# Masked attention, first stage: the high part of the keys cast by ScalarE, the subtraction a slot later, and key stores ahead of key loads

## Chip, cores and metric

One core of a Trainium2 chip (trn2) runs the whole program in one launch. The metric is the device time of one execution in microseconds (us), as the median of several runs.

## The reference, cut to what matters

Eight stages follow each other, each adding to x (32 sequences of 56 rows, width 128). The first one is a cross-attention over 1500 keys a sequence, with 16 heads of width 8, a bias and a mask:

```python
x = x + tanh(g_xattn[0]) * L0_xattn_ref(layernorm(x), ctx, ctx, mask, bias, W_q, b_q, W_k, b_k, W_v, b_v, W_o, b_o)
# in it, for every head: NaN and infinities of q, k, v and the bias are replaced by 0, 10000 and -10000,
# scores = q @ k.T / sqrt(8) + bias, masked keys get -10000, softmax over the keys, times v, times W_o
```

The kernel multiplies q and k to float32's accuracy with bfloat16 operands: q and k are each split into three bfloat16 parts (high, middle, low), and six products of parts are packed into one matmul of 96 rows (`K_PART`, `Q_PART`).

## The kernel before, in words

The change lies in `masked_attention`, the first stage. Its five engines each run a list written out by hand; semaphores order them against each other. The work goes in slots: slot p of sequence n, with p from 0 to 7, treats a pair of heads. In this text "score 4.1" is the scores of slot 4, second half of the keys; "shift 4.1" is VectorE's pass over them; and so on.

What a slot does:
- TensorE: score p.0 (L1017, L1019), transposes of the probabilities' arguments of slot p - 2 (`turn`, L1029), score p.1, more transposes, then one piece of other work: the key projections of sequence n + 2 in slots 0 to 2 (`keys`, L973), the value projections in slots 3 to 5 (`values`, L979), weighted sums (L1042, L1055) in most slots. Score p.h waits for shift (p - 1).h, since the PSUM tile of each half is used again.
- VectorE: shift p.0 (L1310: bias added and the row maximum taken), work on the keys and values of sequence n + 2, shift p.1, more such work, and the negated maximum (L1318).
- ScalarE: three exponentials of slot p - 2 (`exp`, L1141), two subtractions of the maximum (`lower`, L1130), and in slots 0 to 2 the copy of a third of the keys out of PSUM (`keep`, L1124).
- GpSimd: a list with no slots of its own (L945 to L958): guard 0, guard 1, split 0, guard 2, split 1, guard 3, split 2, blocks, guard 4, guard 5. A guard clamps a third of the keys (0 to 2) or of the values (3 to 5) in three operations, L916, L917, L919. A split makes the middle and low part of a third of the keys (L926, L928). `blocks` (L894) lays out the queries.
- SyncE: it issues all DMAs from one queue, in the order of L851 to L872; a wait in it holds all that stands behind.

How a third i of the keys of sequence n + 2 goes on its way, before the change: `keys` (slot i) on TensorE, `keep` on ScalarE, guard i on GpSimd and beside it the finite test `finite` on VectorE (L1257), then `take_keys` in slot i + 2 on VectorE, in one piece: copy i (L1263, the copy under the finite mask), the cast to the high part (L1268), and the subtraction of it, "rest i" (L1270). Before the cast it waits for `k_stored`, since `k_parts` has two buffers for the three thirds: the buffer of third 2 is that of third 0, which must have been stored. Then comes split i, which waits for rest i, then store i (L814), then the loads that pack the keys for the scores (L825), two packed rows at a time, each paced by a count of scores. The packed keys of a half are first read one sequence later.

In slots 2 to 7 VectorE also takes over the values (L1257, L1278, L1285; "copy 3" to "copy 5" below are the values' copies of L1285 in slots 5 to 7, and "copy 4" is that of slot 6, behind guard 4), compares the mask (L1240, slots 0, 2 and 4) and normalises sequence n - 1 (L1338 to L1344, slot 6).

Of the kernel before, what the change touches and what calls it, by code (L numbers as in the profile page):

```python
# [20 lines left out]
ACT = mybir.ActivationFunctionType  # L21
# [673 lines left out]
def masked_attention(nc, g, name, a, w):  # L695
# [4 lines left out]
    with r.ctx:  # L700
# [84 lines left out]
        with nc.Block() as block:  # L785
            @block.sync
            def _(sp):
# [23 lines left out]
                def store_keys(n, i):  # L811
                    at = 3 * n + i
                    sp.wait_ge(low_ready, at + 1)
                    sp.dma_start(a["k_scratch"][n % 2].rearrange("a f k -> f a k")[:, :, third(i)],  # L814
                                 k_parts[:, at % 2, :, :]).then_inc(k_stored[at % 2], 16)
# [35 lines left out]
                for n in range(B):  # L851
                    if n + 1 < B:
                        load_keys(n + 1, 0, (0, 1))
                        load_mask(n + 1, 1)
                        load_keys(n + 1, 0, (2, 3))
                    load_mask_t(n)
                    if n + 1 < B:
                        load_mask(n + 1, 2)
                        load_keys(n + 1, 0, (4, 5))
                    if n > 1:  # L860
                        sp.wait_ge(y_copied, n - 1)
                        sp.dma_start(a["y_scratch"][:, (n - 2) * S:(n - 1) * S], y_now).then_inc(y_stored, 16)
                    for i in range(3):
                        if n + 1 < B:
                            load_keys(n + 1, 1, (2 * i, 2 * i + 1))
                        if n + 2 < B:
                            store_keys(n + 2, i)
                        if n + 3 < B:
                            load_ctx(n + 3, i)
                    if n + 2 < B:  # L870
                        load_mask(n + 2, 0)
                        load_queries(n + 2)  # L872
# [238 lines left out]
            def _(act):  # L1111
# [6 lines left out]
                def keep(n, i):  # L1118
                    at = 3 * n + i
                    act.wait_ge(k_turned, at + 1)  # L1120
                    if at == 0:
                        act.wait_ge(q_ready, NQ)
                    wait(act, k_ready, at - 1)
                    act.activation(raw_k[:, at % 2, :], side[:, 0:THIRD], ACT.Identity, bias=bk[:]).then_inc(raw_k_ready, 1)  # L1124

                def lower(n, p, h):
                    at = n * HP + p
                    act.wait_ge(neg_ready, at + 1)
                    some = logits[at % 3][:, h * HALF:(h + 1) * HALF]
                    act.activation(some, some, ACT.Identity, bias=neg_top[:, n % 2, p:p + 1]).then_inc(lowered, 1)  # L1130
# [32 lines left out]
                    wait(act, y_stored, 16 * n)  # L1163
                    act.activation(y_now, side[:, 0:S], ACT.Identity, bias=bo[:]).then_inc(y_copied, 1)

                for i in range(3):
                    keep(0, i)
                count(0)
                for i in range(3):
                    keep(1, i)  # L1170
                for n in range(B):
                    for p in range(HP):
                        prior = (n, p - 2) if p > 1 else (n - 1, p + HP - 2)
                        last = (n, p - 1) if p > 0 else (n - 1, HP - 1)
                        if p == 0 and n > 1:
                            finish(n - 2)
                        for t in range(3):
                            if prior[0] >= 0:
                                exp(*prior, t)
                            if t < 2 and last[0] >= 0:  # L1180
                                lower(*last, t)
                            if t == 1 and p < 3 and n + 2 < B:
                                keep(n + 2, p)
                        if p == 1 and n > 0:
                            weigh_share(n - 1)
                        if p == 4 and n > 0:
                            mix(n - 1)
                        if p == 5 and n + 1 < B:
                            count(n + 1)
# [11 lines left out]
            def _(dve):  # L1201
# [57 lines left out]
                def take_keys(n, i):  # L1259
                    at = 3 * n + i  # L1260
                    dve.wait_ge(rough_ready, 6 * n + i + 1)
                    dve.wait_ge(good_ready, 6 * n + i + 1)
                    dve.copy_predicated(clean_k[at % 2], good[:, (6 * n + i) % 2, 0:THIRD],  # L1263
                                        raw_k[:, at % 2, :]).then_inc(k_ready, 1)
                    dve.wait_ge(k_ready, at + 1)
                    if at > 1:
                        dve.wait_ge(k_stored[at % 2], 16 * (at // 2))
                    dve.tensor_copy(k_parts[:, at % 2, 0, :], clean_k[at % 2]).then_inc(high_ready, 1)  # L1268
                    dve.wait_ge(high_ready, at + 1)
                    dve.tensor_tensor(clean_k[at % 2], clean_k[at % 2], k_parts[:, at % 2, 0, :],  # L1270
                                      ALU.subtract).then_inc(rest_ready, 1)
# [77 lines left out]
                for n in (0, 1):  # L1349
                    for i in range(3):  # L1350
                        finite(n, i)
                        take(n, i)
                    for b in range(3):
                        keep_values(n, b)
                        finite(n, b + 3)
                        take(n, b + 3)
                    if n == 0:
                        for i in range(3):
                            mark(0, i)
                        clean_bias()  # L1360
                        floors(0)
                for n in range(B):
                    for p in range(HP):
                        shifted(n, p, 0)
                        if p > 1 and n + 2 < B:
                            take(n + 2, p - 2)
                        if 0 < p < 7 and n + 2 < B:
                            finite(n + 2, p - 1)
                        if p in (0, 2, 4) and n + 1 < B:
                            mark(n + 1, p // 2)  # L1370
                        if p == 5:
                            mark_t(n)
                        shifted(n, p, 1)
                        if 3 <= p < 6 and n + 2 < B:
                            keep_values(n + 2, p - 3)
                        if p == 0 and n > 0:
                            share_of(n - 1)
                        if p == 5 and n > 0:
                            add_masked(n - 1)
                        if p == 6 and n > 0:  # L1380
                            normalise(n - 1)
                        if p == 7 and n + 1 < B:
                            floors(n + 1)
                        negate(n, p)
# [1239 lines left out]
```

## Time and profile before

| what | value |
|---|---|
| median of 3 runs | 6507.41 us (6505.57 to 6512.12) |
| time of the profiled execution | 6505.09 us |
| its span | 6503.3 us |
| mean granted TensorE clock | 0.915 |
| busy: TensorE, VectorE, ScalarE, GpSimd | 5399.5, 4556.5, 3155.4, 1967.3 us |
| the loop of the changed stage, first to last shift | 161.7 to 1550.1 us |

The profile is that of one execution. Busy times are sums over all eight stages; the loop of the stage that the change touches is a fifth of the span. In the timelines below a row has the start in us from the beginning of the span, the duration in us, the engine, the line, the operation, what it writes and reads, and, in brackets, how long the engine stood idle just before it and who ended that.

### The profile page before, as it was taken

The page shows a single profiled execution, that of the slowest core. Times are in us where ns is not written, and L with a number is a line of the kernel's source. Part 1 is how long each engine was busy: PE and PEld are TensorE (multiplying, and loading weights), DVE is VectorE, ACT ScalarE, POOL GpSimd, SP SyncE. Part 2 cuts the span into 40 slices and gives each one's busy share as a digit, 9 for nine tenths or more (in the row PEclk, how much of TensorE's full clock was granted, in tenths as well). Part 3 has the DMA queues.
Part 4 walks back from the last instruction along what each step waited for, and adds up shares of the span by engine and source line. Part 5 has one row for each costly group of instructions (what it writes and reads, how often), then busy time and mean ns, then how long its engine had stood idle before and what let it go on. Part 6 is the DMA issues. An engine that isn't in the chain of part 4 may idle for free. (4 is left out here: it accounts for less than half of the span.)

```text
span 6503.3 us, 132525 instructions
## 1 busy us (share of the span) xinstructions
PE 5399.5 (83%) x51199; PEld 3938.7 (61%) x51199; DVE 4556.5 (70%) x9168; ACT 3155.4 (49%) x5932; POOL 1967.3 (30%) x1458
## 2 busy tenths in 40 slices
PE   2898898896599999955947999999999658888887
PEld 1777777775277777745933444444444437777775
DVE  6888888885177777751446777777777448778774
ACT  0666666664165555531224444444444225555552
POOL 4766766761122222201011111111110023333330
PEclk6999999998699999977978999999999769999998
DMA  4555555552366666631010000000000068888870
GB/s 109 124 121 125 122 121 125 122 120 54 75 120 131 133 129 126 132 87 50 23 27 25 15 19 14 14 19 14 14 19 4 5 128 148 143 150 150 146 138 10
DMA packets 368260, 544.58 MB, mean 84 GB/s; under 512 B 115654, under 2 KB 247880, under 8 KB 367390
## 3 DMA queue, kind: packets, MB, share of 16 engines
q1 hardware_dynamic: 365678, 533.44, 39.8%
q8 instruction: 378, 6.19, 0.5%
q0 software_dynamic: 2048, 3.67, 0.2%
q14 instruction: 156, 1.28, 0.1%
HBM read 413.08 MB, written 123.90 MB: 83 GB/s over the span
## 5 line engine op out<-in xcount | busy, mean ns | idle before, releaser
L635 DVE CUSTOM_DVE_ANT_0 attn_logits<-attn_scores,attn_shift 112x750 f32<-112x750 f32 x1024 | 943.5, 931 | 468.4 <-PE attn_scores L452 467.7
L555 ACT ACTIVATE attn_probs_t<-attn_pt 125x448 f32<-125x448 f32 x1536 | 831.2, 542 | 780.4 <-PE attn_pt L467 760.3
L467 PEld LDWEIGHTS attn_pt<-ident,attn_logits 112*125 112x125 f32 x6144 | 867.0, 191 | 222.3 <-issue 80.7
L467 PE MATMUL attn_pt<-ident,attn_logits 112*125 112x112 f32 x6144 | 926.2, 274 | 67.8 <-DVE attn_logits L649 42.1
L2241 PE MATMUL attn2k_pk<-attn_wk,attn2k_cn_t 128*125 128x512 f32 x1536 | 737.9, 602 | 39.5 <-ACT attn2k_cn_t L2312 36.7
L2252 PE MATMUL attn2k_pg<-attn2k_kn,attn2k_cn 125*128 125x512 f32 x1536 | 725.0, 594 | 4.5 <-ACT attn2k_gram L2320 2.3
L2407 DVE TENSOR_REDUCE attn2k_ss<-attn2k_sq 125x16 f32<-125x1024 f32 x384 | 467.0, 1216 | 255.4 <-ACT attn2k_sq L2349 255.3
L389 POOL CAST attn_k_parts<-xn_t 128x500 bf16<-128x500 f32 x192 | 199.4, 1039 | 1407.4 <-DVE xn_t L605 1407.3
L1141 ACT ACTIVATE attn_probs_t<-attn_pt 125x448 f32<-125x448 f32 x768 | 414.8, 540 | 308.5 <-PE attn_pt L1029 305.9
L2349 ACT ACTIVATE attn2k_sq<-attn2k_pk 125x1024 f32<-125x1024 f32 x384 | 391.9, 1021 | 326.3 <-PE attn2k_pk L2241 326.2
L452 PE MATMUL attn_scores<-attn_k_packed,attn_q_blocks 96*112 96x375 bf16 x2048 | 523.3, 338 | 24.6 <-POOL attn_q_blocks L379 17.9
L2241 PEld LDWEIGHTS attn2k_pk<-attn_wk,attn2k_cn_t 128*125 128x125 f32 x1536 | 274.1, 187 | 399.3 <-issue 296.9
L1017 PE MATMUL attn_scores<-attn_k_packed,attn_q_blocks 96*112 96x375 bf16 x1024 | 357.2, 349 | 149.3 <-DVE attn_tops L1310 149.3
L2419 DVE TENSOR_TENSOR attn2k_kn<-attn2k_pk,attn2k_rn 125x1024 f32<-125x1024 f32 x384 | 470.1, 1224 | 13.3
L2252 PEld LDWEIGHTS attn2k_pg<-attn2k_kn,attn2k_cn 125*128 125x128 f32 x1536 | 264.1, 192 | 298.2 <-issue 286.3
L1310 DVE CUSTOM_DVE_ANT_0 attn_logits<-attn_scores,attn_bias,attn_floor 112x750 f32<-112x750 f32 x342 | 337.9, 988 | 101.8 <-PE attn_scores L1019 100.2
L649 DVE TENSOR_SCALAR attn_logits<-attn_logits,attn_neg_top 112x1500 f32<-112x1500 f32 x320 | 375.5, 1173 | 0.1
L480 PE MATMUL attn_po<-attn_probs_t,attn_v 125*32 125x112 f32 x12288 | 371.7, 272 | 1.3 <-ACT attn_probs_t L555 1.3
L1130 ACT ACTIVATE attn_logits<-attn_logits,attn_neg_top 112x750 f32<-112x750 f32 x342 | 312.9, 916 | 113.7 <-DVE attn_neg_top L1318 111.6
L2223 POOL COPY attn2k_q_now<-attn_q_t 128x448 f32 (+1 forms) x32 | 17.8, 558 | 1135.4 <-PE attn2k_pz L2273 1135.4
L546 ACT ACTIVATE attn_logits<-attn_logits,attn_neg_top 112x750 f32<-112x750 f32 x384 | 351.2, 915 | 10.5 <-DVE attn_neg_top L643 8.8
L421 PE MATMUL attn_side<-attn_ctx_t,attn_wk 128*128 128x500 f32 x384 | 219.7, 655 | 152.8 <-DVE xn_t L605 86.1
(360 smaller groups left out, 10814.0 us busy)
## 6 DMA issues: line engine op xcount, KB each, us to landing
attn_k_packed<-k_scratch SPq DMA_DIRECT2D x384, 375.0 KB, 5.9
attn_k_packed<-k_scratch SPq DMA_DIRECT2D x384, 187.5 KB, 3.9
k_scratch<-attn_k_parts SPq DMA_DIRECT2D x64, 1125.0 KB, 7.4
attn_ctx_t<-in_ctx_t SPq DMA_DIRECT2D x64, 750.0 KB, 7.3
k_scratch<-attn_k_parts SPq DMA_DIRECT2D x96, 375.0 KB, 4.5
attn_ctx_t<-in_ctx_t SPq DMA_DIRECT2D x96, 250.0 KB, 4.6
attn2k_ctx<-in_ctx SPq DMA_DIRECT2D x32, 750.0 KB
attn_mask_in<-in_mask SPq DMA_DIRECT2D x192, 109.4 KB
```

What stands on the lines that cost most here:

```text
L452: last = pe.matmul(scores[h][0:PAIR, b, 0:QTR], q_blocks[:, n % 2, p, :, :].rearrange("p a s -> p (a s)"), k_packed[:, n % 2, p, h * HALF ...
L467: last = pe.transpose(pt[(3 * at + t) % 2][0:KC, (c % 4) * PAIR:(c % 4 + 1) * PAIR], logits[:, at % 3, c * KC:(c + 1) * KC], g.ident[0:PAI ...
L480: last = pe.matmul(po[32 * j:32 * j + 32, grp * PAIR:(grp + 1) * PAIR], v[:, n % 3, c, V1 * p:V1 * p + 32], probs_t[0:KC, grp, c, j * PAIR ...
L555: act.activation(probs_t[0:KC, p // 4, 4 * t:4 * t + 4, (p % 4) * PAIR:(p % 4 + 1) * PAIR], pt[(3 * at + t) % 2][0:KC, 0:QUAD].rearrange(" ...
L635: dve.tensor_tensor_reduce(out=logits[:, at % 3, cols].rearrange("p (b k) -> p b k", b=2), in0=scores[h][0:PAIR, :, 0:QTR], in1=shift[:, n ...
L649: dve.tensor_scalar(at, at, neg_top[:, n % 2, p:p + 1], None, ALU.add).then_inc(dve_lowered, 1)
L1141: act.activation(probs_t[0:KC, at % PV_RING, 4 * t:4 * t + 4, :], pt[(3 * at + t) % 2][0:KC, 0:QUAD].rearrange("p (c q) -> p c q", c=4), A ...
L2241: last = pe.matmul(pk[c % 2][0:KC, b, :], cn_t[:, c % 2, :], wk[:, b * HW:(b + 1) * HW], start=True, stop=True)
L2252: last = pe.matmul(pg[:, b, :], cn[:, j, c, :], kn[:, c % 2, b * HW:(b + 1) * HW], start=(c == 0), stop=(c == CH - 1))
L2349: act.activation(sq[:, c % 2, :].rearrange("p (a b) -> p a b", a=2), pk[c % 2][0:KC, :, :], ACT.Square).then_inc(sq_ready, 1)
L2407: dve.tensor_reduce(ss[:, c % 2, :], sq[:, c % 2, :].rearrange("p (h d) -> p h d", h=H2), AX.X, ALU.add).then_inc(ss_ready, 1)
L2419: dve.tensor_tensor(kn[:, c % 2, :].rearrange("p (h d) -> p h d", h=H2), pk[c % 2][0:KC, :, :].rearrange("p a (h d) -> p (a h) d", h=8), r ...
```

## The change

In `take_keys`, VectorE's cast and the wait for `k_stored` ahead of it go away. A new function `high` does both on ScalarE, with an activation of type Copy; in the loop it stands at the end of slots 2, 3 and 4, after the third exponential. VectorE's subtraction becomes a function of its own, `rest`, and stands behind shift p.0 in slots 3, 4 and 5, ahead of the copy of that slot: one slot later than before. In the prologue ScalarE's list is laid out anew, with the same idea. On SyncE, store i of sequence n + 2 goes ahead of the two key loads of sequence n + 1 with which it shares a step of the loop.

```diff
@@ sync
                     for i in range(3):
+                        if n + 2 < B:
+                            store_keys(n + 2, i)
                         if n + 1 < B:
                             load_keys(n + 1, 1, (2 * i, 2 * i + 1))
-                        if n + 2 < B:
-                            store_keys(n + 2, i)
                         if n + 3 < B:
                             load_ctx(n + 3, i)
@@ scalar
+                def high(n, i):
+                    at = 3 * n + i
+                    act.wait_ge(k_ready, at + 1)
+                    if at > 1:
+                        act.wait_ge(k_stored[at % 2], 16 * (at // 2))
+                    act.activation(k_parts[:, at % 2, 0, :], clean_k[at % 2], ACT.Copy).then_inc(high_ready, 1)
...
-                for i in range(3):
-                    keep(0, i)
-                count(0)
-                for i in range(3):
-                    keep(1, i)
+                for n in (0, 1):
+                    keep(n, 0)
+                    keep(n, 1)
+                    high(n, 0)
+                    keep(n, 2)
+                    high(n, 1)
+                    high(n, 2)
+                    if n == 0:
+                        count(0)
...
+                        if 2 <= p < 5 and n + 2 < B:
+                            high(n + 2, p - 2)
@@ vector
-                    dve.wait_ge(k_ready, at + 1)
-                    if at > 1:
-                        dve.wait_ge(k_stored[at % 2], 16 * (at // 2))
-                    dve.tensor_copy(k_parts[:, at % 2, 0, :], clean_k[at % 2]).then_inc(high_ready, 1)
+
+                def rest(n, i):
+                    at = 3 * n + i
                     dve.wait_ge(high_ready, at + 1)
                     dve.tensor_tensor(clean_k[at % 2], clean_k[at % 2], k_parts[:, at % 2, 0, :],
                                       ALU.subtract).then_inc(rest_ready, 1)
...
                         take(n, i)
+                        rest(n, i)
...
                         shifted(n, p, 0)
+                        if 3 <= p < 6 and n + 2 < B:
+                            rest(n + 2, p - 3)
                         if p > 1 and n + 2 < B:
                             take(n + 2, p - 2)
```

## Rows read from the trace of the kernel before

**Rows 1.** The page, part 1: busy time, share of the span, instructions.
```profile
PE 5399.5 (83%) x51199; PEld 3938.7 (61%) x51199; DVE 4556.5 (70%) x9168; ACT 3155.4 (49%) x5932; POOL 1967.3 (30%) x1458
```

**Rows 2.** Windows: length, busy of PE, PEld, DVE, ACT, POOL, granted clock; one sequence.
```profile
850.70:856.40 5.70, 5.64 (x36) 4.88 (x36) 5.57 (x11) 3.02 (x5) 5.62 (x5) 0.50 0.32 95
...
sum 44.30, PE 39.55 PEld 33.95 DVE 37.52 ACT 28.96 POOL 30.32; mean PE 7.91 PEld 6.79 DVE 7.50 ACT 5.79 POOL 6.07
```

**Rows 3.** Waits, 400 to 1400 us: us in total, times, longest.
```profile
PE attn_scores L1017 <- DVE attn_tops L1310: 110.5, 67, 4.4
...
DVE attn_k_parts L1268 <- DMA k_scratch<-attn_k_parts: 40.2, 23, 2.4
```

**Rows 4.** Timeline of TensorE: scores 2.0, 3.0, 5.1, then 0.1, 3.0 of the next.
```profile
831.16 0.37 PE L1017 MATMUL attn_scores<-attn_k_packed,attn_q_blocks 96*112 96x375 bf16 x1
...
836.00 0.37 PE L1017 MATMUL attn_scores<-attn_k_packed,attn_q_blocks 96*112 96x375 bf16 x1
...
850.76 0.56 PE L1017 MATMUL attn_scores<-attn_k_packed,attn_q_blocks 96*112 96x375 bf16 x1 [3.84 <-DVE attn_tops L1310]
...
866.83 0.32 PE L1017 MATMUL attn_scores<-attn_k_packed,attn_q_blocks 96*112 96x375 bf16 x1
...
880.31 0.37 PE L1017 MATMUL attn_scores<-attn_k_packed,attn_q_blocks 96*112 96x375 bf16 x1
```

**Rows 5.** Timeline of VectorE, slots 2 to 7 of the same sequence.
```profile
832.05 1.00 DVE L1310 CUSTOM_DVE_ANT_0 x_sb<-attn_scores,attn_bias,attn_floor 112x750 f32<-112x750 f32 x1 [2.14 <-PE attn_scores L1019]
...
833.75 1.31 DVE L1268 CAST attn_k_parts<-attn_clean_late 128x500 bf16<-128x500 f32 x1
...
840.82 1.47 DVE L1257 TENSOR_SCALAR attn_good<-xn_t 128x500 int32<-128x500 f32 x1
...
844.77 0.97 DVE L1263 COPY_PREDICATED attn_clean_late<-attn_good,xn_t 128x500 f32<-128x500 int32 x1
847.26 0.75 DVE L1268 CAST attn_k_parts<-attn_clean_late 128x500 bf16<-128x500 f32 x1 [1.51 <-DMA k_scratch<-attn_k_parts]
...
849.71 0.98 DVE L1310 CUSTOM_DVE_ANT_0 attn_logits<-attn_scores,attn_bias,attn_floor 112x750 f32<-112x750 f32 x1
...
851.35 0.98 DVE L1310 CUSTOM_DVE_ANT_0 x_sb<-attn_scores,attn_bias,attn_floor 112x750 f32<-112x750 f32 x1
...
858.73 0.77 DVE L1285 COPY_PREDICATED attn_v<-attn_good,y_t 125x512 f32<-125x512 int32 x1
...
865.16 0.98 DVE L1310 CUSTOM_DVE_ANT_0 attn_logits<-attn_scores,attn_bias,attn_floor 112x750 f32<-112x750 f32 x1
```

**Rows 6.** Line L1268, whole stage: durations in ns, min/median/max, first and last start.
```profile
L1268 DVE CAST attn_k_parts<-xn_t x48: 420/472/1321, 49.6 to 1461.0; 128x500 bf16<-128x500 f32 x48
```

**Rows 7.** Timeline of ScalarE: key copy and last exponentials of slots 2 and 4.
```profile
835.02 0.68 ACT L1124 ACTIVATE xn_t<-attn_side,attn_bk 128x500 f32<-128x500 f32 x1
835.58 0.55 ACT L1141 ACTIVATE attn_probs_t<-attn_pt 125x448 f32<-125x448 f32 x1
...
846.03 0.53 ACT L1141 ACTIVATE attn_probs_t<-attn_pt 125x448 f32<-125x448 f32 x1
```

**Rows 8.** Timeline of SyncE's queue: store 0.
```profile
842.85 0.42 SPq L814 DMA_DIRECT2D k_scratch<-attn_k_parts  x1
```

**Rows 9.** Timeline of GpSimd: split 0, ends of guards 2 and 3, split 2, end of guard 4.
```profile
835.84 0.72 POOL L926 CAST attn_k_parts<-attn_clean_late 128x500 bf16<-128x500 f32 x1 [1.06 <-DVE attn_clean_late L1270]
...
840.73 1.29 POOL L919 TENSOR_TENSOR attn_clean_late<-attn_clean_late,y_t 128x500 f32<-128x500 f32 x1
...
846.55 1.18 POOL L919 TENSOR_TENSOR attn_v<-attn_v,y_t 125x512 f32<-125x512 f32 x1
...
848.79 0.73 POOL L926 CAST attn_k_parts<-attn_clean_late 128x500 bf16<-128x500 f32 x1 [1.06 <-DVE attn_clean_late L1270]
...
855.45 1.19 POOL L919 TENSOR_TENSOR attn_v<-attn_v,y_t 125x512 f32<-125x512 f32 x1
```

**Rows 10.** Line L1270, whole stage: durations in ns, min/median/max, first and last start.
```profile
L1270 DVE TENSOR_TENSOR xn_t<-xn_t,attn_k_parts x48: 678/680/1489, 50.3 to 1461.5; 128x500 f32<-128x500 f32 x48
```

## The prediction

> **What bounds the kernel now.** The page comes first. TensorE is busy 83% of the span, VectorE 70% [rows 1]; that average mixes eight stages, and the change touches one, the first attention with its 32 sequences. So the page can't price it. The windows over one of its sequences can: 44.30 us, in which TensorE is busy 39.55, VectorE 37.52, GpSimd 30.32 and ScalarE 28.96 [rows 2]. No engine is full, so a chain through several of them sets the period. The waits say where it breaks: score matmuls (L1017) waited 110.5 us in 1000 us for VectorE's shift pass, and VectorE's cast waited 40.2 us, 23 times, for the key store to land [rows 3].
>
> The timelines of one sequence give the chain. Score 3.0 (slot 3, first half) starts at 836.00 and again at 880.31, a period of 44.31. From 821.4 to slot 5 TensorE runs almost through; then it stands 3.84 us until score 5.1 at 850.76 [rows 4], and the granted clock is at its lower level, 0.50 (1.2 of 2.4 GHz), for the next 5.7 us [rows 2]. It stood for shift 4.1, which VectorE began at 849.71 only, because it had waited 1.51 us for the store, then cast for 0.75 and subtracted for 0.68 [rows 5]. After score 5.1 TensorE runs without a gap to score 3.0 of the next sequence, the last 13.48 us of it from score 0.1 at 866.83. Shift 7.1, which score 0.1 needs, ended at 866.14 [rows 4, 5]: VectorE's second chain has only 0.69 us to spare. That slack matters below.
>
> **The change, part by part.** Only the 30 sequences that prepare keys for n + 2 change.
>
> *Cast off VectorE.* Three casts a sequence, 0.42 us at the least and 1.32 at the most, median 0.47 [rows 6], and the store's wait of 1.51. In slot 4 it is 1.51 + 0.75 = 2.26 us ahead of shift 4.1, and the subtraction beside it moves in front of the copy. In slot 2 the gain is smaller than it looks: the cast lasted 1.31 instead of 0.42 because it started under a GpSimd operation [rows 5], and the finite test that now takes its place would start under the same one and end at the same 835.06. The mask compare then takes 0.4, and shift 2.1 starts at 835.4 instead of 836.76, so score 3.1 waits no longer.
>
> *Cast on ScalarE.* No row has it. The nearest is the key copy L1124, also 128x500, at 0.68 us [rows 7]; below, VectorE's own 0.42 [rows 6]; I take 0.65. Three are 1.95 us on an engine that is idle 15 us of 44.30. Each stands behind the last exponential of its slot: high 0 comes when that ends at 836.13, and high 2, whose exponential ends at 846.56 [rows 7] (about 845.2 after the change, since slot 4 begins earlier), when copy 2 is done at 845.7. Each is done well before its subtraction in the next slot; what queues behind high 2 is the mix and exp 3.0, at most 0.65 us later, while TensorE stands waiting for shift 4.1. Cost zero. Without that cover it would be at most 0.65 a sequence.
> The Trainium skill (ScalarE: Activation LUTs, What ACT_TABLE_LOAD costs) gives an ACTIVATE with immediate scale and bias 186 ns plus 0.833 ns an element, an estimate of 0.60 us here, which would change nothing in the sum.
>
> *Stores ahead of loads.* SyncE issued store 0 at 842.85, behind two key loads that are paced by the scores; the cast could go on at 847.26, 4.41 later [rows 8, 5]. Now it goes when the low part is ready, at about 840.6 by the next step, and lands at 845.0, before high 2 at 845.7 wants its buffer. Loads 4 and 5 may wait up to 1 us longer behind store 2, but slot 4 of the next sequence is some 40 us away. Cost zero, gain already counted.
>
> *The subtraction a slot later.* This is what costs. Shift 3.0 starts 0.89 after score 3.0, as shift 2.0 did (831.16 to 832.05 [rows 4, 5]): 836.89. Rest 0 ends 0.91 + 0.68 later, at 838.48, and GpSimd can begin split 0 at 838.54 instead of 835.84 [rows 9]: 2.70 late. GpSimd's order is fixed: split 0, guard 2, split 1, guard 3, split 2, blocks, guard 4. That took 835.84 to 856.64, less an idle of 1.06: 19.74 us of work [rows 9]. Before, the guards had room; now they follow on each other:
> - guard 2 ends at 842.02 + 2.70 = 844.72, so copy 2 in slot 4 starts at 844.8, where it stood before (844.77). It ends at 845.7; finite test and mask compare then cost 0.42 each alone and up to 1.47 beside GpSimd [rows 5]. Between 846.8 and 848.2 for shift 4.1, I take 847.9: 1.8 us gained.
> - Shift 5.0 follows 1.64 later (849.71 to 851.35 [rows 5]), 849.5; rest 2 could start at 850.4, just when guard 3 makes its last, two-input operation (846.55 to 847.73 before [rows 9], now about 849.4 to 850.6). A subtraction took 1.49 at the most, against a median of 0.68 [rows 10], and the long ones are those of the prologue that met such an operation. So rest 2 ends between 851.1 and 851.9, and GpSimd, free at 850.5, waits 0 (if shift 4.1 comes early) to 1.4 us; I take 0.9.
> - guard 4 ends at 838.54 + 19.74 + 0.9 = 859.2, and copy 4 starts at 859.3. It started at 858.73 [rows 5]: 0.57 late. VectorE had gained 1.8 and loses all of it at this point.
> - Copy 4 to the end of shift 7.1 took 7.41 [rows 5]. Guard 5 now runs beside the normalisation: 0 to 0.5 more, I take 0.2. Shift 7.1 ends at 866.91, score 0.1 starts at 866.98, score 3.0 another 13.48 later, at 880.46.
>
> **Sum.** 880.46 - 836.00 = 44.46 against 44.31: +0.15 us, times 30 is +4.5 us. The profiled execution took 6505.1 us, so 6509.6 for one like it; the median of the three runs lies 2.3 above it: 6512. All that the edits save goes into the 0.69 us of slack and into GpSimd's later start.
> Bounds: without any collision and wait, copy 4 is at 858.35, the period 43.3, that is -1.0 x 30 = -30 us: 6477. With GpSimd waiting 1.4, 0.5 more inside its operations and 0.5 in the normalisation, the period is 45.7, +1.4 x 30 = +42: 6549.
>
> The row on the subtraction is mixed: 1.49 at the most, yet 0.68 in the median [rows 10]; but then most ran while GpSimd waited for them, so it says little of a GpSimd that is always busy. The Trainium skill (SBUF — State Buffer, Who interferes with whom) has VectorE and GpSimd share one port pair as an exclusive lock, a two-input VectorE operation meeting any GpSimd operation that reads. By that rule rest 1 and rest 2 are both held, and the time is that of the slower case below; the longest subtraction speaks for it, the median neither way.
>
> **The rivals.**
> - *Faster, chance 0.25.* VectorE's two-input and fast operations fall between GpSimd's, shift 4.1 comes at 846.8 and rest 2 is done before GpSimd asks. Then the period is 43.3 to 43.8. For it: 40.2 us of waits and all the casts are truly gone. Against: GpSimd is busy without a gap for 20 us, so collisions are hard to miss. About 43.6, -0.7 x 30: 6486.
> - *GpSimd does not bind at all, 0.05.* Then shift 4.1's full 2.26 comes through, -68 us: 6440. Against it is the fixed order.
> - *Slower, 0.30: GpSimd's chain in slot 6.* Place: copy 4 waits for guard 4. Price: every us that rest 0 or rest 2 comes late, times 30. It decides once copy 4 starts after 859.2, since 0.69 less the 0.2 for normalisation is used up at that time. With a period of 45.1, +0.8 x 30: 6531.
> - *A second low clock, 0.04.* TensorE could reach score 7.1 at 860.1 and waits for shift 6.1 until 861.3; if that idle brings the lower level again where TensorE sets the end, it costs as in [rows 2] half of 5.7 us, 86 us in all: 6598. Idles of 0.5 did not do it, 3.84 did.
> - *The wait only moves*: if store 0 landed after 845.7, ScalarE would wait instead. Rest 2 has 4 us of room for it, so it is worth nothing and is part of the forecast.
>
> **How the numbers follow.** About 0.2% (13 us) can be told from no change, that is 0.43 us a sequence. My forecast, a period within that of 44.31, has 0.36 and gives 6512 (its own range 6495 to 6520). The two faster cases make 0.30, the two slower 0.34. The range 6477 to 6549 leaves out the non-binding case, the second clock fall and the tails, under 0.2 together.
>
> **What would show it.** In the changed profile: no wait of VectorE on the store; casts of 0.6 to 0.68 on ScalarE; shift 4.1 1 to 3 us earlier against score 3.0; GpSimd without idle from split 0 to guard 4, and split 0 about 2.5 us later; a new wait of VectorE in slot 6 before copy 4, on GpSimd; TensorE's wait before score 5.1 down to some 3 us, and a new one before score 7.1 or 0.1. I am wrong if copy 4 does not wait (then faster), if score 0.1 waits over 0.6 us (then slower), or if the low clock stretch goes or doubles.

## The result, and the profile after

The changed kernel took **6583.69 us** (median of 4 runs, 6577.45 to 6589.56), against 6509.76 for the kernel before beside it: a ratio of **1.0111**, 95% interval 1.0097 to 1.0125. That is 1.1% slower and above the range of the prediction (6477 to 6549). The profiled execution took 6577.45 us, its span is 6575.6.

The 72.3 us by which the span grew (6575.6 less 6503.3) lie in the changed stage. VectorE's smallest mask operation (L1245 before, L1258 after) runs once a sequence, in slot 5. From its first to its last run it was 1349.6 us before and is 1423.3 now, 73.7 more. Before, 29 sequences took 44.31 us each on average. Now the shortest take 46.0, and 9 take 46.4. Another 7 take 47.9, the first 46.7, and the step after these 29 takes 39.3 instead of 31.9. So 49 us come from the sequences' shortest period (29 x 1.69), 17.4 from the longer ones, 7.3 from the last step.

The busy times hardly changed (compare [rows 1]). Page, part 1, after:

```profile
PE 5430.0 (83%) x51199; PEld 3956.7 (60%) x51199; DVE 4553.7 (69%) x9072; ACT 3195.5 (49%) x6028; POOL 2006.0 (31%) x1458
```

For VectorE that evenness hides something. Windows from the first to the last shift, before and after (columns as in [rows 2]):

```profile
161.70:1550.10 1388.40, 1239.33 (x18758) 1063.99 (x18762) 1158.75 (x2313) 913.01 (x1546) 912.57 (x751) 0.92 0.53 119
162.30:1623.00 1460.70, 1267.95 (x18764) 1080.26 (x18768) 1159.82 (x2224) 947.13 (x1636) 950.79 (x751) 0.93 0.55 113
```

Before, 68.9 of VectorE's 1158.8 us were its 90 casts. They are gone, and it is still busy 1159.8 us: its other operations became about 70 us longer in all. GpSimd, with the same operations, is busy 38 us longer. So the change added more than idle time: operations of both engines grew.

Windows over one sequence of 46.0 us, from score 3.0 to the next one (the columns are those of [rows 2]):

```profile
840.30:847.10 6.80, 6.72 (x40) 5.68 (x41) 6.80 (x11) 4.10 (x6) 6.03 (x5) 0.52 0.80 152
847.10:854.20 7.10, 5.18 (x76) 4.42 (x74) 4.97 (x13) 3.84 (x8) 6.74 (x6) 1.00 0.94 180
...
sum 46.00, PE 40.44 PEld 34.22 DVE 37.33 ACT 30.17 POOL 31.64; mean PE 6.74 PEld 5.70 DVE 6.22 ACT 5.03 POOL 5.27
```

The lower clock (0.52) is still there in slot 5. In this sequence it lasts 6.8 us, as it did before in every one (now it is 3.4 in most of the others, there or in slot 6), and VectorE is busy through all of it. In the 7.1 us behind it, slot 6, VectorE works for only 4.97 and TensorE for 5.18, while GpSimd works for 6.74. One of the sequences of 47.9 us has the lower clock (0.56 on average) in another place too, from about where its score 7.1 starts (430.47), after a wait of 1.96 us:

```profile
429.60:436.40 6.80, 5.93 (x62) 5.11 (x63) 6.66 (x13) 2.56 (x4) 2.85 (x2) 0.56 0.14 33
```

The waits from 400 to 1400 us say who is waited for (us in total, times, longest):

```profile
PE attn_scores L1017 <- DVE attn_tops L1322: 123.9, 60, 2.9
POOL attn_k_parts L926 <- DVE xn_t L1282: 48.3, 22, 3.8
POOL attn_k_parts L926 <- DVE attn_clean_late L1282: 47.8, 22, 3.8
DVE attn_v L1297 <- POOLq L921: 44.0, 21, 2.1
DVE xn_t L1276 <- POOLq L921: 16.4, 11, 1.5
```

VectorE's wait for the key store, 40.2 us in [rows 3], is gone. In its place VectorE waits for GpSimd: 2.1 us ahead of every copy 4 (L1297) and 1.5 us ahead of every copy 2 (L1276). TensorE's wait for the shift grew from 110.5 to 123.9.

The same sequence in the timelines. TensorE, scores 3.0, 5.1, 7.1, 0.1 and the next 3.0:

```profile
827.86 0.37 PE L1017 MATMUL attn_scores<-attn_k_packed,attn_q_blocks 96*112 96x375 bf16 x1
...
840.38 0.56 PE L1017 MATMUL attn_scores<-attn_k_packed,attn_q_blocks 96*112 96x375 bf16 x1 [2.92 <-DVE attn_tops L1322]
...
854.25 0.37 PE L1017 MATMUL attn_scores<-attn_k_packed,attn_q_blocks 96*112 96x375 bf16 x1 [1.96 <-DVE attn_tops L1322]
...
860.37 0.32 PE L1017 MATMUL attn_scores<-attn_k_packed,attn_q_blocks 96*112 96x375 bf16 x1
...
873.84 0.37 PE L1017 MATMUL attn_scores<-attn_k_packed,attn_q_blocks 96*112 96x375 bf16 x1
```

VectorE: shift 3.0, rests 0 and 1, copy 2, shift 4.1, rest 2, a mask operation, copy 4, one step of the normalisation, shift 7.1:

```profile
828.75 1.00 DVE L1322 CUSTOM_DVE_ANT_0 attn_logits<-attn_scores,attn_bias,attn_floor 112x750 f32<-112x750 f32 x1 [0.35 <-PE attn_scores L1019]
829.67 0.68 DVE L1282 TENSOR_TENSOR xn_t<-xn_t,attn_k_parts 128x500 f32<-128x500 f32 x1
...
834.55 0.68 DVE L1282 TENSOR_TENSOR attn_clean_late<-attn_clean_late,attn_k_parts 128x500 f32<-128x500 f32 x1
836.72 0.72 DVE L1276 COPY_PREDICATED xn_t<-attn_good,xn_t 128x500 f32<-128x500 int32 x1 [1.50 <-POOLq L921]
...
839.33 0.99 DVE L1322 CUSTOM_DVE_ANT_0 x_sb<-attn_scores,attn_bias,attn_floor 112x750 f32<-112x750 f32 x1
...
841.89 1.68 DVE L1282 TENSOR_TENSOR xn_t<-xn_t,attn_k_parts 128x500 f32<-128x500 f32 x1
...
844.87 1.44 DVE L1258 TENSOR_SCALAR attn_out_t<-attn_out_t 125x672 f32<-125x672 int32 x1
...
851.80 0.77 DVE L1297 COPY_PREDICATED attn_v<-attn_good,y_t 125x512 f32<-125x512 int32 x1 [2.10 <-POOLq L921]
...
855.69 0.87 DVE L1352 TENSOR_TENSOR xn_t<-attn_mixed,xn_t 128x224 f32<-128x224 f32 x1
...
859.09 0.97 DVE L1322 CUSTOM_DVE_ANT_0 x_sb<-attn_scores,attn_bias,attn_floor 112x750 f32<-112x750 f32 x1
```

GpSimd: split 0, the long step of guard 2, split 1, the end of guard 3, split 2, the end of guard 4:

```profile
830.41 1.00 POOL L926 CAST attn_k_parts<-xn_t 128x500 bf16<-128x500 f32 x1 [3.80 <-DVE xn_t L1282]
...
833.42 1.88 POOL L917 TENSOR_SCALAR xn_t<-xn_t 128x500 f32<-128x500 f32 x1
...
836.80 1.06 POOL L926 CAST attn_k_parts<-attn_clean_late 128x500 bf16<-128x500 f32 x1 [0.17 <-POOL xn_t L919]
...
841.85 1.18 POOL L919 TENSOR_TENSOR attn_v<-attn_v,y_t 125x512 f32<-125x512 f32 x1
843.63 1.04 POOL L926 CAST attn_k_parts<-xn_t 128x500 bf16<-128x500 f32 x1 [0.60 <-DVE xn_t L1282]
844.75 1.19 POOL L928 TENSOR_TENSOR attn_k_parts<-xn_t,attn_k_parts 128x500 bf16<-128x500 f32 x1
...
850.53 1.19 POOL L919 TENSOR_TENSOR attn_v<-attn_v,y_t 125x512 f32<-125x512 f32 x1
```

GpSimd stands still for 3.80 us until rest 0 is done, then works to the end of guard 4 at 851.72, with one wait on VectorE, 0.60 us for rest 2. Copy 4 starts 0.08 us after that end.

The two moved pieces did what they were meant to. The cast on ScalarE, whole stage (ns, min/median/max), and store 0 on SyncE's queue:

```profile
L1131 ACT ACTIVATE attn_k_parts<-xn_t x48: 621/626/635, 50.2 to 1528.2; 128x500 bf16<-128x500 f32 x48
```

```profile
832.72 0.38 SPq L814 DMA_DIRECT2D k_scratch<-attn_k_parts  x1
```

### The profile page after: what moved, and what is told of

Same layout as the page of the kernel before. It is cut to its first block and busy times, and to the rows that moved or that the text cites. A ratio compares the mean times of both kernels' runs of the same rounds, so it can differ in the third digit from the quotient of the medians.

```text
span 6575.6 us, 132525 instructions
## 1 busy us (share of the span) xinstructions
PE 5430.0 (83%) x51199; PEld 3956.7 (60%) x51199; DVE 4553.7 (69%) x9072; ACT 3195.5 (49%) x6028; POOL 2006.0 (31%) x1458
```

## The experiments

The theories, as the expectations name them. **A**: GpSimd's fixed list starts a slot later, because the subtraction does, and comes out too late at copy 4. **B**: the stores' new place on SyncE's queue costs (SyncE waits for the low part with loads behind it). **C**: ScalarE's cast holds up the exponentials. **D**: the cost lies in the collisions of VectorE and GpSimd, each lengthening the other's operations, and not in the date at which GpSimd starts.

"VectorE's cast" below is the cast of the kernel before, "late" is the subtraction one slot later. Ratios are against runs of the kernel before on the same chip (medians 6510.65 to 6512.86).

**One part alone: the store order.** The kernel before with each store ahead of the two key loads. Since the subtraction stays early, store 0 now could overwrite packed keys that are still being read, so SyncE also waits for that read ahead of store 0.

```diff
                     for i in range(3):
+                        if n + 2 < B:
+                            if i == 0:
+                                sp.wait_ge(k_in[(2 * n + 1) % 3], ((2 * n + 1) // 3 + 1) * NPART * 16)
+                            store_keys(n + 2, i)
                         if n + 1 < B:
                             load_keys(n + 1, 1, (2 * i, 2 * i + 1))
-                        if n + 2 < B:
-                            store_keys(n + 2, i)
```

> The kernel before with SyncE's order alone changed (store i ahead of its two key loads; one wait for key loads that were done some 30 us earlier is added ahead of store 0). Theory A, GpSimd's list begins a slot later because of the late subtraction: this part is innocent; VectorE's wait of 1.5 us before the cast of slot 4 goes, shift 4.1 comes up to 1.5 us earlier, GpSimd's list is not later, so the time is between no change and -45 us (1.5 x 30): about 6490. Theory B, the stores' waits hold SyncE's queue and the key loads come late: slower than before, up to the full +73 us, with waits of score matmuls on key loads in the trace. Theory C, ScalarE's cast holds the exponentials: no part of it is here, so as theory A.

Measured: 6464.93 us, ratio 0.9927 (0.9908 to 0.9946). It is **faster than both kernels**, and theory B falls. The wait for the store is gone and GpSimd's list still starts early. Waits, 400 to 1400 us:

```profile
PE attn_scores L1019 <- DVE attn_tops L1312: 94.7, 75, 3.0
...
POOL attn_k_parts L928 <- DVE xn_t L1272: 12.7, 12, 1.1
```

TensorE waits 94.7 us where it was 110.5 [rows 3], and no wait of VectorE for GpSimd appears.

**The other part alone: the subtraction a slot later.** The kernel before, stores in their old place, cast on VectorE.

```diff
+                def rest(n, i):
+                    at = 3 * n + i
                     dve.wait_ge(high_ready, at + 1)
...
                         shifted(n, p, 0)
+                        if 3 <= p < 6 and n + 2 < B:
+                            rest(n + 2, p - 3)
```

> The kernel before with the subtraction alone moved a slot later; the cast stays on VectorE in the slot of the copy, the stores stay behind the loads. Theory A: slower than before, by at least as much as the changed kernel, since VectorE keeps its casts and its waits: +60 to +120 us, 6570 to 6630, with VectorE waiting for GpSimd before copy 2 (slot 4) and copy 4 (slot 6). Theory B and theory C: within 0.3% of before, since neither ScalarE nor SyncE's order is touched; a store's wait may even be shorter.

Measured: 6591.91 us, ratio 1.0131 (1.0106 to 1.0155). This one edit costs as much as the whole change. The same waits stand there as after the change: VectorE's for GpSimd ahead of copy 4 in the same amount (44.0 us), GpSimd's for the rests somewhat longer (112.5 us against 96.1):

```profile
POOL attn_k_parts L926 <- DVE attn_clean_late L1273: 56.9, 33, 3.8
POOL attn_k_parts L926 <- DVE xn_t L1273: 55.6, 32, 3.8
DVE attn_v L1288 <- POOLq L921: 44.0, 21, 2.1
```

**The change with the subtraction back in its slot.** Cast on ScalarE behind the second `lower` of the slot, rest i in slot i + 2 behind the finite test and the mask, ahead of shift p.1; the same wait ahead of store 0.

```diff
-                        if 3 <= p < 6 and n + 2 < B:
-                            rest(n + 2, p - 3)
...
+                        if 2 <= p < 5 and n + 2 < B:
+                            rest(n + 2, p - 2)
```

> The changed kernel with the subtraction back in the slot of its copy, behind the finite test and the mask compare and ahead of the second shift; ScalarE casts one step earlier in its slot, after the second lowering (and the one extra wait for key loads as in the store order alone). Theory A: GpSimd starts split 0 within about 1 us of the kernel before, copies 2 and 4 wait no longer, and VectorE is rid of cast and store wait: faster than before by 0.5 to 2 us a sequence, 6450 to 6495. Theory B and theory C: cast on ScalarE and store order are both in it, so it stays as slow as the changed kernel, about 6580.

Measured: 6519.88 us, ratio 1.0018 (1.0007 to 1.0029). A miss for A as it was put: the change's loss is gone, the gain of the store order isn't there. ScalarE's way round is longer than VectorE's own cast, so split 0 is still 1.1 us later than before against shift 3.0 (table below). VectorE waits for GpSimd again:

```profile
DVE attn_v L1299 <- POOLq L923: 61.4, 46, 2.1
```

**The layout of the queries behind the guards.** The changed kernel, with GpSimd's `blocks` after guards 4 and 5, so that guard 4 is free to end earlier.

```diff
-                    if n + 1 < B:
-                        blocks(n + 1)
                     if n + 2 < B:
                         guard(n + 2, 4)
                         guard(n + 2, 5)
+                    if n + 1 < B:
+                        blocks(n + 1)
```

> The changed kernel with GpSimd's blocks operation (1.7 to 1.9 us, needed only by the next sequence) moved behind guards 4 and 5. Theory A: guard 4 ends some 1.9 us earlier, VectorE's wait of 2.1 us before copy 4 goes to about 0.2, and the period falls by 1.0 to 1.9 us: 30 to 57 us off the changed kernel, 6525 to 6555. Theory B and theory C: GpSimd is not the bound, the time stays at about 6582 within 0.2%.

Measured: 6604.3 us, ratio 1.0130 (1.0107 to 1.0154). A miss, and not for want of the first effect: copy 4's wait fell from 2.10 to 0.44. But the layout now meets the normalisation, whose second two-input step (L1354, 0.39 us after the change) waits it out. Timeline of VectorE, then of GpSimd, then of TensorE:

```profile
855.37 0.81 DVE L1297 COPY_PREDICATED attn_v<-attn_good,y_t 125x512 f32<-125x512 int32 x1 [0.44 <-POOLq L921]
...
860.18 1.88 DVE L1354 TENSOR_TENSOR attn_mixed<-xn_t 128x224 int32<-128x224 f32 x1
```

```profile
860.14 1.68 POOL L894 TENSOR_TENSOR attn_q_blocks<-x_sb,attn_row_head 96x896 bf16<-96x896 bf16 x1 [0.24 <-POOL attn_v L919]
```

```profile
862.62 1.45 PE L1002 MATMUL attn_side<-xn_t,attn_wo 128*128 128x56 f32 x8 [1.78 <-DVE xn_t L1356]
```

So the collisions of theory D are real and have a price of 1.5 us in one place. That takes back most of the 1.8 us by which copy 4 comes earlier, and no more: shift 7.1 still ends 0.26 us earlier than in the change (table below). What makes this kernel the slower one lies behind that. TensorE now waits 1.8 us for the normalisation ahead of its output projection (L1002), and in 17 of 29 sequences the granted clock is at the lower level for 6.8 us from about there. These 17 take 48.2 to 48.7 us, the other 12 at most 45.8, less than the change's 46.0. What shares the two theories have in the change itself was open, and the next seven runs were for that and for the rest of the table.

**The three runs that complete the table.** The changed kernel with the old store order; the late subtraction with VectorE's cast and the new order; ScalarE's cast in the same slot with the old order. Each undoes one edit shown above; the extra wait ahead of store 0 stands in every kernel with the new store order except the changed one.

> The changed kernel with the stores back behind the two key loads: only the late subtraction and ScalarE's cast are left of the change. Theory A (GpSimd's list starts a slot later and comes out at copy 4 too late): the store order buys nothing here, since no cast waits for a store when the cast itself is asked for late; the same as the changed kernel, 6575 to 6600. Theory B (the stores' place on SyncE's queue is what costs): back near the kernel before, 6500 to 6530. Theory C (ScalarE's cast holds the exponentials): as the changed kernel, or a little slower if high 2 now waits for store 0.

> The changed kernel with the cast back on VectorE, behind the copy: stores first and the subtraction a slot later. Theory A: GpSimd starts as late as in the changed kernel, 6570 to 6600, although the two halves of the edit are both there and the store order alone gave 48 us. Theory C: with ScalarE free of the casts it falls under 6540. Theory B has no case left after the store order alone was faster.

> The kernel before with the cast alone moved to ScalarE: the subtraction stays in its slot, stores behind the loads. The same-slot kernel with the stores first took 6520, and the store order alone 6465, so ScalarE's cast in the same slot cost about 55 us. Theory A: the cost is that split 0 comes some 0.6 us later than before, and the stores' order adds to it, so 6520 to 6580. Theory D (the cost lies in the collisions of VectorE with a GpSimd that is never idle, not in the date of its start): about 6520, as with the stores first.

Measured: 6582.16 (1.0113, 1.0098 to 1.0127), 6584.53 (1.0110, 1.0095 to 1.0125) and 6508.3 (0.9994, 0.9985 to 1.0003). In the third, A and D both expected more; without the late subtraction, ScalarE's cast is as good as VectorE's, and the wait for the store moves to ScalarE (37.7 us in 1000, the longest 2.9). That the new store order makes this one 0.2% slower and not faster was not taken apart. The start of GpSimd's list doesn't explain it: split 0 is equally late with both orders, yet VectorE's waits for GpSimd are 3.4 us in 1000 with the old order and 61.4 with the new one, where shift 5.0 comes earlier and split 2 later (table below). The whole table, as ratios to the kernel before:

| cast | stores | subtraction in its slot | a slot later |
|---|---|---|---|
| VectorE | behind the loads | 1 | 1.0131 |
| VectorE | ahead | **0.9927** | 1.0110 |
| ScalarE | behind | 0.9994 | 1.0113 |
| ScalarE | ahead | 1.0018 | 1.0111 (the change) |

In the right column, cast and store order make no difference beyond the intervals; in the left they do. A gain upstream that does not come through is what one expects where something else sets the date. Theory C has no case: with VectorE's cast the late kernels are no faster. (Their sequences without a second stretch of the lower clock take 46.5 to 46.8 us, against 46.0 with ScalarE's cast. But at most 1 of 29 has such a stretch of 6.8 us, where 8 and 9 have it with ScalarE's cast; see below.)

**GpSimd's list late by other means.** The kernel before, with two and with three idle operations of GpSimd ahead of split 0, on its scratch tile. They add work to GpSimd and delay its list; VectorE's and ScalarE's lists are untouched.

```diff
+                        pool.wait_ge(rest_ready, 3 * (n + 2) + 1)
+                        for t in (1, 2):
+                            pool.tensor_tensor(below[:, 0:THIRD], below[:, 0:THIRD], below[:, 0:THIRD], ALU.add).then_inc(idle_steps, 1)
+                            pool.wait_ge(idle_steps, 2 * n + t)
                         split(n + 2, 0)
```

> The kernel before, in which GpSimd does two extra two-input operations of about 1.3 us each on its scratch tile ahead of split 0 of every sequence; nothing else is touched. Theory A: a GpSimd list that starts about 2.6 us later is the whole cost of the change, so this is as slow as the late subtraction alone, 6560 to 6610. If it stays within 15 us of the kernel before, the start of GpSimd's list does not bind, and the cost of the late subtraction is in VectorE's own order. Theory C and B: no change, 6505 to 6520.

> The kernel before with three extra GpSimd operations ahead of split 0 instead of two. With two, split 0 came 1.94 us later against shift 3.0 and the kernel took 32 us more, without a wait of VectorE for GpSimd; with the late subtraction split 0 comes 3.75 us later and the kernel takes 85 us more. The slack of copy 4 on guard 4 in the kernel before is about 2.1 us. Theory A (the date of GpSimd's list decides once it passes that slack): split 0 is some 3.2 us late, copy 4 waits for guard 4 for about 1 us, and the step from two to three costs more than the first two did each: 6575 to 6600. Theory D (collisions alone, in proportion to GpSimd's extra work): 16 us more for the third, 6555 to 6565, without a wait at copy 4.

Measured: 6544.25 (1.0046, 1.0034 to 1.0058) with two, 6593.19 (1.0129, 1.0114 to 1.0144) with three. The two cost 32 us, the third alone some 50. The kernel before forgives some of the delay, and then no more. With two, copy 4 still waits for nothing; with three it waits (VectorE's timeline):

```profile
855.15 0.81 DVE L1290 COPY_PREDICATED attn_v<-attn_good,y_t 125x512 f32<-125x512 int32 x1 [0.43 <-POOLq L922]
```

But the wait is 0.43 us and not the expected 1, and copy 2 waits 0.60. VectorE itself reaches copy 4 later, for its operations on the way became longer: the mask operation of slot 5 takes 0.50 us before, 0.91 with two idle operations and 1.98 with three (medians). So a late list costs through both, D's collisions and A's wait. The time lies where A had put it (6575 to 6600), but of the 2.3 us by which copy 4 comes later after score 3.0 only 0.43 are the wait.

**GpSimd's list shortened in the changed kernel.** Guard 4 in one operation instead of three; it leaves out the handling of NaN in a third of the values. All else is the changed kernel.

```diff
+                    if i == 4 and n > 1:
+                        pool.tensor_scalar(to, raw, MASKED, -MASKED, ALU.max, ALU.min).then_inc(rough_steps, 1)
+                        pool.wait_ge(rough_steps, done + 1)
+                        pool.sem_inc(rough_steps, 2)
```

> The changed kernel with guard 4 of every sequence in the loop in one GpSimd operation instead of three: it leaves out the handling of NaN in a third of the values. GpSimd has some 2.1 us less to do right ahead of copy 4, which waited 2.10 us for it. Theory A (GpSimd's date at copy 4 is the bound): copy 4 starts 2.1 us earlier, the period falls from 46.0 by 1.4 to 2.1, 6505 to 6535. Theory D (collisions in slots 3 to 7 lengthen VectorE's own work, the wait only absorbs the rest): guard 5 now meets the normalisation, and the kernel stays over 6550.

Measured: 6511.75 us, ratio 1.0002 (0.9993 to 1.0010), 72 us less than the changed kernel. Copy 4 in VectorE's timeline:

```profile
855.04 0.79 DVE L1304 COPY_PREDICATED attn_v<-attn_good,y_t 125x512 f32<-125x512 int32 x1 [0.20 <-POOLq L921]
```

The wait is 0.20 instead of 2.10. Nothing ahead of copy 4 moved (table below), the way from copy 4 to the end of shift 7.1 still took 8.3 us, and the period fell from 46.0 to 44.1, by the same 1.9 us by which copy 4 came earlier. This is theory A in its plainest form: in the changed kernel the end of guard 4 sets the time. It doesn't say what made guard 4 late (see below), and the kernel before with the same shortening wasn't run. The longer sequences went too: all but the first, shorter one lie between 44.1 and 44.5.

**The same reordering where copy 4 doesn't wait.** The store order alone, with `blocks` behind the guards.

> The store order alone (6465 us) with GpSimd's layout of the queries behind guards 4 and 5. Copy 4 doesn't wait for GpSimd there, so theory A sees nothing to gain: 6460 to 6475, unless the layout meets the normalisation as it did in the changed kernel (theory D), which would cost up to 1.5 us a sequence: up to 6510.

Measured: 6468.62 us, ratio 0.9937 (0.9924 to 0.9950): nothing to tell it from the store order alone. VectorE isn't held by GpSimd's date there, so moving it buys nothing.

Where the dates lie, medians over 20 sequences, in us after the start of shift 3.0. The second column says how long after score 3.0 that shift itself starts; added to a date, it gives the date after score 3.0.

| kernel | shift 3.0 | split 0 | split 2 | shift 5.0 | copy 4 | end of shift 7.1 | period |
|---|---|---|---|---|---|---|---|
| before | 1.91 | -2.08 | 10.89 | 13.45 | 20.82 | 28.24 | 44.37 |
| store order alone | 1.91 | -2.08 | 10.20 | 12.64 | 19.24 | 26.65 | 42.52 |
| ScalarE's cast, same slot, stores ahead | 1.43 | -1.01 | 12.77 | 11.11 | 21.01 | 29.28 | 44.48 |
| ScalarE's cast, same slot, stores behind | 1.43 | -1.01 | 12.17 | 12.11 | 20.65 | 28.95 | 44.15 |
| two idle operations | 2.33 | -0.14 | 12.39 | 14.06 | 21.44 | 28.97 | 45.11 |
| three idle operations | 2.33 | 0.96 | 14.61 | 14.04 | 22.69 | 30.99 | 47.09 |
| the change | 0.89 | 1.67 | 14.89 | 12.23 | 23.06 | 31.32 | 46.38 |
| the change, `blocks` last | 0.89 | 1.67 | 14.89 | 12.23 | 21.27 | 31.06 | 48.21 |
| the change, guard 4 short | 0.89 | 1.67 | 14.89 | 12.23 | 21.16 | 29.46 | 44.14 |

Shift 5.0 is VectorE's progress in the middle of the sequence. It is earlier in the change than before, by 1.22 (by 2.24 after score 3.0). It says nothing about the period. Copy 4, counted after score 3.0, does: it runs from 21.15 to 25.02 as the period runs from 42.5 to 47.1, in the same order but for 0.1 us between two neighbours. The one exception is `blocks` last, with its collision and its lower clock behind copy 4. Counted so, split 0 is 2.73 us later in the change, 2.36 with two idle operations and 3.46 with three.

## Why the prediction was wrong

Its mechanism was right and it gave it the right name: the slower rival, "GpSimd's chain in slot 6", with 0.30, is what happened, and beyond the price that it had. Point by point, in the sequence from 827.86:

- *Cast off VectorE, onto ScalarE*: right. 0.62 to 0.65 us where 0.65 was taken, no wait that matters (3.8 us twice, 11 times each, in 1000 us). The estimate of 0.60 from the Trainium skill (ScalarE: Activation LUTs, What ACT_TABLE_LOAD costs) is 0.03 below the median of 0.626. Shift 2.1 starts 0.71 before score 3.0, as against 0.6 in the forecast.
- *Stores*: right for the change, where store 0 goes out as split 0 ends (832.70) and nobody waits for it. But the working priced only the two edits together. Each alone would have told more: the store order is worth -48 us, and the late subtraction takes that and 73 more.
- *GpSimd starts later*: right. Split 0 was to come 2.54 after score 3.0 (838.54 less 836.00) and came 2.55 after it.
- *Shift 4.1*: expected 11.9 after score 3.0, measured 11.47. VectorE is ahead of the forecast here, and it is worth nothing.
- **The step that failed: "guard 4 ends at 838.54 + 19.74 + 0.9 = 859.2".** The 19.74 was GpSimd's work in a sequence where other VectorE operations fell beside it. From 830.41 to 851.72 are 21.31 us, less the 0.60 of waiting 20.71: GpSimd's own operations became 0.97 longer. Split's cast (L926) takes 1.00 to 1.06 where [rows 9] had 0.72, and `blocks` takes 1.94, where it took 1.68. Rest 2 did collide, in full (1.68 us), but GpSimd waited only 0.60 for it. Copy 4 came 23.94 after score 3.0, against 23.3 forecast.
- **The second term that failed: copy 4 to the end of shift 7.1, "7.41, I take 0.2" more.** It is 8.26 (851.80 to 860.06), 0.85 more. Guard 5 now runs all along it: the finite test takes 0.81 where it took 0.44, and the step L1352 takes 0.87 where it took 0.39. Together 0.85.
- *The end*: score 0.1 started 0.31 behind shift 7.1's end and not 0.07, and the last stretch took 13.47, as the 13.48 forecast. The sum: 0.64 + 0.65 + 0.24 make 1.53, and 44.46 + 1.53 = 45.99, against the 45.98 measured.
- *What of it is the late start*: against the kernel before, guard 4 ends 3.22 later after score 3.0. That is 2.71 for the start of split 0, 0.97 for GpSimd's longer operations, and 0.60 of waiting for rest 2 where it was 1.06. Copy 4 had 2.09 of slack before and starts 0.08 behind guard 4 now, so it comes 1.21 later. By these numbers, as an estimate, guard 4 would have ended within the slack without the 0.97 and the 0.60 (2.71 - 1.06 = 1.65): the late start and the longer operations made the loss together. No run took the two apart.
- *The upper bound* of the period, 45.7, nearly held, by luck: its terms for GpSimd's operations and for the normalisation were 0.5 each, where 0.97 and 0.85 were found, but it allowed 1.4 of waiting for rest 2, where 0.60 was found. Their sum fits (2.4 against 2.42), and the 0.24 at score 0.1 is what passed it: 0.28 a sequence, 8 us. Nearly all the rest of the 35 us above 6549 is what one period times 30 can't hold: 17.4 us from sequences that are longer than the shortest one, for which it had no term but the rival below, and 7.3 from the last step.
- *A second low clock*, 0.04: it came, in part. In all 7 sequences of 47.9 us the granted clock is at the lower level for 6.8 us from about score 7.1 on, in all 9 of 46.4 us for 3.4 us from there, and in the 12 of 46.0 us not at all from there to slot 3 of the next. (The first, of 46.7 us, is of the first kind.) So they make the 17.4 us. The wait ahead of score 7.1 is where the rival put it, 1.96 us in all of these. In the run with guard 4 short that wait doesn't stand there, and no sequence has the lower clock in that place. Of the 12 sequences of 46.0 us, 5 wait only 0.4 there, and 4 of the other 7 had the lower clock in slot 5 for 6.8 us, where all 16 with the second stretch had it for 3.4. Why the same wait brings it in some sequences and not in others stays open beyond that.
- The 7.3 us of the last step weren't taken apart.

The place where the sum was most sure of itself was the one to doubt. It carried two lengths over unchanged, GpSimd's 19.74 and VectorE's 7.41, though the change shifts the two engines against each other, by 3.75 us at split 0 against shift 3.0. The prediction named the collisions and put them into the bounds at 0.5 us each, for which no row stood; into the forecast it put only 0.2 for the normalisation and nothing for GpSimd's own operations.

**Which operations collide.** The rest that begins on top of GpSimd's two-input operation (841.85) takes 1.68 instead of 0.68, about what is left of that operation plus its own time. So it is in all 30 places of this kind (1.67 to 1.69). Rest 1 at 834.55 lies wholly beside GpSimd's one-input operation L917 (833.42 to 835.30) and takes 0.68, and so in 31 places (0.67 to 0.68). One input is not what spares it: in the kernel before, a rest of the prologue that began at 137.38, beside GpSimd's other one-input operation, L916 (137.24 to 137.84), took 0.99. The mask operation at 844.87 begins beside the two-input L928 and takes 1.44, where it took 0.50 before. The Trainium skill (SBUF — State Buffer, Who interferes with whom) says that a VectorE instruction with two SBUF inputs contends with any GpSimd instruction that reads SBUF. The traces agree for rest 2 and, with `blocks` last, for L1354 beside the layout (1.88 us), and disagree for rest 1: the measurement decides, and the rule's forecast that both rests are held was half right.

## What to carry to other kernels

Where an engine runs a fixed list, a step that feeds the head of that list is not free to move, even if the step's own date is never late: ask how much later the last item of the list comes out, who waits for that, and how much slack it had (here 2.1 us, used up by a start 2.7 us later and operations that grew by 1.0). And where a change shifts two engines that share something against each other, no length measured on either carries over as it is. Last, price each edit of a change alone: here one part of it was worth 0.7% on its own, and another hid that and took 1.1% besides.

## What had not been expected of the hardware

- GpSimd's operations change their length with what VectorE does beside them: its cast from 0.72 to 1.06 us, its layout of the queries from 1.68 to 1.94. The list as a whole grew by 5% (19.74 to 20.71), though not one of its operations was changed.
- The price of one more operation of 1.1 us on GpSimd was some 50 us in 30 sequences, about 1.7 us a sequence, more than its own length (three idle operations against two): VectorE's mask operation in slot 5 alone went from 0.91 to 1.98 us.
- VectorE's operations with two inputs waited behind GpSimd's two-input ones (0.68 to 1.68, 0.39 to 1.88) but not behind its long one-input operation L917 (0.68); beside the short one, L916, one of them took 0.99.
